# A four-stage fused kernel: attention's weighted sums taken from fp32 probabilities and values, with VectorE's and GpSimd's work re-ordered by key range

## The chip, the cores and the metric

One core of one Trainium2 chip runs the whole program. The metric is the time of one execution in microseconds of device time; the figure compared is the median over runs. Engines are named as in the profile: PE (TensorE's matmuls), PEld (its weight loads), DVE (VectorE), ACT (ScalarE), POOL (GpSimd), SP (SyncE, which issues DMAs here).

## The reference

Four layers one after the other, each followed by a layer norm, on x of shape [8, 512, 128] in fp32: banded attention, a routed feed-forward with 16 experts (4 per token), a linear attention with decay, and a routed feed-forward with 8 experts (2 per token). The change touches the first layer alone:

```python
qkv = jnp.einsum('bld,ed->ble', xn, w_qkv).reshape(B, L, 3, H, HD)      # H = 16 heads of HD = 8
scores = jnp.einsum('bhqd,bhkd->bhqk', q, k) / jnp.sqrt(jnp.float32(HD))
band = jnp.abs(idx[:, None] - idx[None, :]) <= WINDOW // 2              # 16 keys to either side
scores = jnp.where(band[None, None], scores, -jnp.inf)
attn = jax.nn.softmax(scores, axis=-1)
out = jnp.einsum('bhqk,bhkd->bhqd', attn, v)
return residual + jnp.einsum('bld,ed->ble', out, w_out)
```

## The kernel before, in words

The engines' programs are written by hand, one block per engine, and they meet only at semaphores, so the order of the code is the order on each engine. Attention runs over 8 batches; `over_attention` writes batches 0 and 1 out, loops over batches 2 to 5, and writes 6 and 7 out. The argument `prev` of `body` is 0 for batch 0, 1 for batch 1, and 2 from batch 2 on, when the routing of batch b - 2 runs beside attention of batch b. `nxt` says that there is a batch b + 1 to prepare.

A batch has five key ranges ("range" below, `w` in the code): 128 keys each (`WIN`) and 112, 96, 96, 96 and 112 queries (`NQ`), 512 in all. The 16 heads stand in 4 groups `g` of 4 heads `t`. For each range:

- PE makes transposed scores in `t_bank` for groups 0 and 1, later 2 and 3 (`scores_t`: products of `kst` and `qst`, then the mask and the row maximum from `lay` and `mov`). A second form of the scores (`scores`, in `s_bank`) serves only for the maxima: DVE reduces them (`max_of`, L798) and splits them (`split_max`), PE turns them (`turn_max`) and ACT lays them out (`lay_max`, L1224).
- ACT takes the exponential twice, into fp32 (`prob`, L1229) and into bf16 (`prob_hi`, L1230). The low part `prob_lo`, the difference, is formed by DVE for groups 0 and 2 (`prob_low`, L804) and by POOL for groups 1 and 3 (`low_of`, L595).
- PE forms weighted sums and denominators (`weighted`, L1527): for each group five rounds of four products, one round per operand pair: high probabilities with high and with low values, low probabilities with high values, and both parts with a block of ones. The four products of a round are the four heads; each has 128 rows and 32 columns of the array, at column position 32 t. All add up in the bank `avbank`.
- DVE divides (`divide`: reciprocal L824, product L825) and counts `ao_ready`, for which the next range's first `weighted` waits.

The order on PE in a range is: `scores_t` of groups 0 and 1, `scores` (ranges 0, 1 and 4), `weighted` of the range before for groups 2 and 3, other work, `scores_t` of groups 2 and 3, other work, `weighted` of this range for groups 0 and 1, `turn_max`, other work. The other work is the next batch's projections in fp32 (`stacks`, L1448, eight per batch of 512 columns, each followed by an ACT cast L1210 and a DVE merge L780), its values, the output projection of the batch before (L1538), and the transposes and logits of its routing (L1616, L1622). DVE also normalises (L987), ranks (`weigh`, `place`), and POOL issues 16 indirect DMAs per batch that scatter the rows of batch b - 2 into the experts' regions (`scatter`, L634), and makes the low parts of the experts' weights (L621).

The values are kept in bf16, high and low, in `v2`; DVE makes the low part from PSUM (`value_low`, L790, five instructions per batch).

After the last batch SP fills the experts' regions' tails (L474) and waits for the scatters; then the first expert stage begins.

## Time and profile before

| | us |
|---|---|
| median of 3 runs | 1188.61 (1185.93 to 1189.94) |
| the profiled execution | 1178.28 |
| its span, first to last instruction | 1176.3 |
| attention's stretch, first weighted sum to last | 49.0 to 416.1 |

The span is what the engines' rows add up in; the profiled execution's own time has 2.0 us around it. The profile cuts the span into rows by engine, line and tile; "idle before" is time in which the engine had nothing running before an instruction of that group, with what ended it. A PE instruction's end is modelled, so the start-to-start distance of PE rows says more than their durations.

### The profile page before, as it was taken

The page shows a single profiled execution, that of the slowest core. Times are in us where ns is not written, and L with a number is a line of the kernel's source. Part 1 is how long each engine was busy: PE and PEld are TensorE (multiplying, and loading weights), DVE is VectorE, ACT ScalarE, POOL GpSimd, SP SyncE. Part 2 cuts the span into 40 slices and gives each one's busy share as a digit, 9 for nine tenths or more (in the row PEclk, how much of TensorE's full clock was granted, in tenths as well). Part 3 has the DMA queues.
Part 4 walks back from the last instruction along what each step waited for, and adds up shares of the span by engine and source line. Part 5 has one row for each costly group of instructions (what it writes and reads, how often), then busy time and mean ns, then how long its engine had stood idle before and what let it go on. Part 6 is the DMA issues. An engine that isn't in the chain of part 4 may idle for free.

```text
span 1176.3 us, 36298 instructions
## 1 busy us (share of the span) xinstructions
PE 816.6 (69%) x12246; PEld 626.6 (53%) x12247; DVE 746.2 (63%) x2119; ACT 548.4 (47%) x1350; POOL 639.9 (54%) x645
## 2 busy tenths in 40 slices
PE   3889787687887620888888788825756618999920
PEld 1456454455545520766767676614544517988820
DVE  4677878587776750556555666547887635666656
ACT  2577656555565610544444445502323215666623
POOL 1145477585856875355545555524767662555533
PEclk9898868778787655899899999967676758999975
DMA  6011111111111213322223332232342222222233
GB/s 187 12 30 38 33 45 48 30 54 38 56 36 43 61 56 102 69 60 60 62 61 65 67 68 64 54 108 75 99 137 93 75 79 61 64 59 52 54 122 111
DMA packets 135796, 79.02 MB, mean 67 GB/s; under 512 B 104338, under 2 KB 116793, under 8 KB 135696
## 3 DMA queue, kind: packets, MB, share of 16 engines
q1 hardware_dynamic: 121808, 50.97, 17.6%
q0 software_dynamic: 13312, 25.31, 6.8%
q8 instruction: 71, 1.16, 0.4%
q10 hardware_dynamic: 576, 1.34, 0.3%
q14 instruction: 29, 0.24, 0.1%
HBM read 32.34 MB, written 32.63 MB: 55 GB/s over the span
## 4 chain that ended last, share of the span: by engine, by line
PE 46%; issue 15%; DVE 14%; ACT 7%; POOL 6%; another core or an unknown queue 5%; SPq 3%; DMA 2%; ACTq 1%; DVEq 0%; POOLq 0%
PE avbank L1679 5%; PE proj L1679 5%; POOL xs L634 4%; PE proj L1448 3%; PE t L1660 3%; PE s L1658 2%; PE t L1659 2%; PE t L1658 2%; ACT act_out L1334 2%; PE t L1513 2%; PE s L1659 2%; PE t L1724 2%; PE s L1660 2%; PE avbank L1527 2%
## 5 line engine op out<-in xcount | busy, mean ns | idle before, releaser
L700 POOL DMA_INDIRECT yt<-ysb,to_now x224 | 235.2, 1050 | 240.8 <-ACT ysb L1321 181.2
L634 POOL DMA_INDIRECT xs<-x1p,sidx x192 | 194.3, 1012 | 55.0 <-issue 47.2
L944 DVE CAST h_hi<-act_out 128x512 bf16<-128x512 f32 x152 | 72.5, 477 | 146.2 <-ACT act_out L1334 123.6
L595 POOL TENSOR_TENSOR prob_lo<-prob,prob_hi 128x384 bf16<-128x384 f32 (+1 forms) x80 | 78.7, 984 | 91.8 <-ACT prob_hi L1230 90.6
L1658 PE MATMUL s<-xt,w_hi 128*128 128x256 bf16 x296 | 82.8, 280 | 54.3 <-DMA xt<-xs 45.6
L945 DVE TENSOR_TENSOR h_lo<-act_out,h_hi 128x512 bf16<-128x512 f32 x152 | 107.8, 709 | 5.2
L1229 ACT ACTIVATE prob<-t 128x384 f32<-128x384 f32 (+1 forms) x160 | 82.0, 513 | 36.1 <-PE t L1513 34.7
L1334 ACT ACTIVATE act_out<-t,b_sb 128x256 f32<-128x256 f32 x152 | 62.0, 480 | 60.0 <-remote 51.2
L1679 PE MATMUL avbank<-w_hi,h_hi 128*128 x448 | 84.8, 222 | 4.9 <-issue 3.6
L1659 PE MATMUL s<-xt,w_hi 128*128 128x256 bf16 x296 | 82.8, 280 | 6.5 <-issue 6.5
L1660 PE MATMUL s<-xt,w_lo 128*128 128x256 bf16 x296 | 82.9, 280 | 5.5 <-issue 5.5
L1679 PE MATMUL proj<-w_hi,h_hi 128*128 x448 | 82.8, 221 | 5.1 <-DVE h_lo L945 2.5
L1679 PE MATMUL avbank<-w_lo,h_hi 128*128 x448 | 82.1, 220 | 2.8 <-issue 2.8
L1659 PE MATMUL t<-xt,w_hi 128*128 128x256 bf16 x296 | 81.8, 277 | 1.6 <-issue 1.6
L1679 PE MATMUL avbank<-w_hi,h_lo 128*128 x448 | 82.5, 220 | 0.6 <-issue 0.6
L1658 PE MATMUL t<-xt,w_hi 128*128 128x256 bf16 x296 | 81.8, 277 | 1.3 <-issue 1.2
L1660 PE MATMUL t<-xt,w_lo 128*128 128x256 bf16 x296 | 81.8, 276 | 0.9 <-issue 0.8
L1230 ACT ACTIVATE prob_hi<-t 128x384 bf16<-128x384 f32 (+1 forms) x160 | 82.3, 514 | 0.0
L1679 PE MATMUL proj<-w_lo,h_hi 128*128 x448 | 81.1, 220 | 1.6 <-issue 1.6
L1679 PE MATMUL proj<-w_hi,h_lo 128*128 x448 | 81.0, 220 | 0.5 <-issue 0.5
L804 DVE TENSOR_TENSOR prob_lo<-prob,prob_hi 128x384 bf16<-128x384 f32 (+1 forms) x80 | 71.4, 892 | 15.1 <-ACT prob_hi L1230 12.5
L798 DVE TENSOR_REDUCE nm<-s 128x8 f32<-128x512 f32 x64 | 41.2, 685 | 49.6 <-PE s L1476 49.4
(230 smaller groups left out, 2396.5 us busy)
## 6 DMA issues: line engine op xcount, KB each, us to landing
w_raw<-w_all SPq DMA_DIRECT2D x56, 256.0 KB
gat<-yt SPq DMA_DIRECT2D x8, 1024.0 KB
gat<-yt SPq DMA_DIRECT2D x8, 512.0 KB, 4.5
yt<-ysb,to_now POOLq DMA_INDIRECT x224
xs<-tail_rows SPq DMA_DIRECT2D x24, 129.0 KB
xs<-x1p,sidx POOLq DMA_INDIRECT x192
out<-ow SPq DMA_DIRECT2D x8, 256.0 KB, 2.4
xt<-xs SPq DMA_TRANSPOSE x112, 2.9
```

The source lines that it names most:

```text
L595: pool.tensor_tensor(prob_lo[:, g, 0:width], prob[:, g, 0:width], prob_hi[:, g, 0:width], ALU.subtract).then_inc(low_odd, 1)
L634: pool.indirect_dma_start(out=xs[n][:, :], out_offset=bass.IndirectOffsetOnAxis(sidx[:, par, at:at + 1], 0), in_=x1p[:, par, t, k, :], in_ ...
L700: pool.indirect_dma_start(out=yt[n][:, :], out_offset=bass.IndirectOffsetOnAxis(to_now[:, u, s:s + 1], 0), in_=ysb[:, u, s, :], in_offset= ...
L944: ch.link(dve.tensor_copy(h_hi[:, par, c, :], act_out[:, par, c, :]))
L945: dve.tensor_tensor(h_lo[:, par, c, :], act_out[:, par, c, :], h_hi[:, par, c, :], ALU.subtract).then_inc(split_done[n], 1)
L1229: nc.scalar.activation(prob[:, g, 0:width], t_bank[g % 2][:, 0:width], ACT.Exp, scale=SCALE)
L1230: nc.scalar.activation(prob_hi[:, g, 0:width], t_bank[g % 2][:, 0:width], ACT.Exp, scale=SCALE).then_inc(exp_done, 1)
L1334: ins = nc.scalar.activation(act_out[:, par, c, :], h_bank[2 * par + c // 2][:, (c % 2) * TILE:(c % 2 + 1) * TILE], ACT.Gelu, bias=b1_sb[: ...
L1658: pe.matmul(dst, w_h, xt[:, u, 0, :], start=True, stop=False)
L1659: pe.matmul(dst, w_h, xt[:, u, 1, :], start=False, stop=False)
L1660: return pe.matmul(dst, w_l, xt[:, u, 0, :], start=False, stop=True)
L1679: ins = pe.matmul(dst, x[:, par, c, rows], w, start=(n == 1 and c == 0 and m == 0 and k == 0), stop=True, skip_group_check=True)
```

## The change

The probabilities are kept only as `prob` in fp32, the values only as `vf` in fp32, and the ones too. ACT takes one exponential per group instead of two; `prob_low` on DVE, `low_of` on POOL and `value_low` on DVE are gone; `weighted` issues two rounds of four products with fp32 operands instead of five with bf16 ones. `exp_done` takes the place of the semaphores of the low parts. DVE's list is written in another order: `divide` comes first in each range, the maxima and the other work behind it, and `weigh` and `place` go from range 0 to the end of range 1's list. POOL's scatters go from ranges 1 to 4 (one row block each) to ranges 2, 3 and 4 (one, one and two row blocks); `rstd_of_y` and `rstd_of` come ahead of them.

```diff
@@ tiles
-        v2 = sb("v2", [P, 2, NW, 4, VT], BF16)
-        one_of = sb("one_of", [P, G * 5 * HD], BF16)
+        vf = sb("vf", [P, 2, NW, 4, G * VG])
+        one_of = sb("one_of", [P, G * 5 * HD])
-        prob_hi = sb("prob_hi", [P, G, 4 * P], BF16)
-        prob_lo = sb("prob_lo", [P, G, 4 * P], BF16)
@@ gpsimd
-            def low_of(win, w, g):
-                pool.wait_ge(exp_done, G * win + g + 1)
-                width = 4 * NQ[w]
-                pool.tensor_tensor(prob_lo[:, g, 0:width], prob[:, g, 0:width], prob_hi[:, g, 0:width],
-                                   ALU.subtract).then_inc(low_odd, 1)
...
                 for w in range(NW):
-                    low_of(b * NW + w, w, 1)
-                    if prev == 2 and w > 0:
-                        if w == 1:
+                    if w == 1 and prev:
+                        rstd_of_y(b)
+                    if w == 2 and nxt2:
+                        rstd_of(b + 2)
+                    if prev == 2 and w > 1:
+                        if w == 2:
                             pool.wait_ge(slots_ready[0], b - 1)
                             pool.wait_ge(x1_spread, b - 1)
                             apart(pool)
-                        scatter(0, par, w - 1, range(0, K0 // 2))
-                    low_of(b * NW + w, w, 3)
...
+                        for t in ((0,), (1,), (2, 3))[w - 2]:
+                            scatter(0, par, t, range(K0))
@@ vector
-            def value_low(b, par):
...
-            def prob_low(win, w, g):
...
                 for w in range(NW):
                     win = b * NW + w
-                    if w < 2:
-                        max_of(b, 1, 2 * w)
-                        max_of(b, 1, 2 * w + 1)
-                    if w == 1:
-                        split_max(b, 1)
-                    if w == 4 and nxt:
-                        max_of(b + 1, 0, 0)
-                        max_of(b + 1, 0, 1)
-                    prob_low(win, w, 0)
                     if w > 0 or prev:
                         beside = None
                         if w == 0 and prev == 2:
                             beside = lambda: take_ranks(0, b - 2, rk_ps)
                         divide(win - 1, (w - 1) % NW, par if w > 0 else 1 - par, beside)
...
+                    if w < 2:
+                        max_of(b, 1, 2 * w)
+                        max_of(b, 1, 2 * w + 1)
+                    if w == 0:
+                        stack(0, 1)
+                    if w == 1:
+                        if prev:
+                            residual(b - 1)
+                        split_max(b, 1)
+                        stack(2)
+                        if prev:
+                            residual_stats(b - 1)
+                        stack(3)
+                        if prev == 2:
+                            weigh(0, b - 2)
+                            place(0, b - 2, par)
...
@@ scalar
-                nc.scalar.activation(prob[:, g, 0:width], t_bank[g % 2][:, 0:width], ACT.Exp, scale=SCALE)
-                nc.scalar.activation(prob_hi[:, g, 0:width], t_bank[g % 2][:, 0:width], ACT.Exp,
+                nc.scalar.activation(prob[:, g, 0:width], t_bank[g % 2][:, 0:width], ACT.Exp,
                                      scale=SCALE).then_inc(exp_done, 1)
@@ tensor
-                pe.wait_ge((low_even, low_odd)[g % 2], 2 * win + g // 2 + 1)
+                pe.wait_ge(exp_done, G * win + g + 1)
                 nq = NQ[w]
                 ones = one_of[:, 4 * HD * g:4 * HD * g + 4 * HD]
-                for dst, part, x in ((num_ps, 0, prob_hi), (num_ps, 4 * HD, prob_hi), (num_ps, 0, prob_lo),
-                                     (den_ps, None, prob_hi), (den_ps, None, prob_lo)):
+                for dst in (num_ps, den_ps):
                     for t in range(4):
                         ins = pe.matmul(dst[32 * t:32 * t + 32, 0:nq],
-                                        ones if part is None else value_block(par, w, t, g, part),
-                                        x[:, g, t * nq:(t + 1) * nq],
-                                        start=g == 0 and x is prob_hi and part == 0, stop=True,
+                                        value_block(par, w, t, g) if dst is num_ps else ones,
+                                        prob[:, g, t * nq:(t + 1) * nq],
+                                        start=g == 0 and dst is num_ps, stop=True,
                                         skip_group_check=True, tile_position=(0, 32 * t))
```

On DVE this is what stands at ranges 0 and 1 of batch 6 (`qst<-hi,cf,proj` is a stack's merge, `nm<-s` the maxima, `rden` and `ao_t` the division, `msum` to `sidx` are `weigh` and `place`). Before, range 0:

```order
L798 TENSOR_REDUCE nm<-s 128x2x4 x2
L804 TENSOR_TENSOR prob_lo<-prob,prob_hi 128x448
L863 TENSOR_TENSOR r<-avbank,cf 128x64
L824 RECIPROCAL rden<-avbank 128x112
L97 ISA
L825 TENSOR_TENSOR ao_t<-avbank,rden 128x112
L804 TENSOR_TENSOR prob_lo<-prob,prob_hi 128x448
L780 SCALAR_TENSOR_TENSOR qst<-hi,cf,proj 128x512 x2
L870 TENSOR_REDUCE msum<-mask 128x16
```

And in the changed kernel, ranges 0 and 1 of the same batch:

```order
L831 TENSOR_TENSOR r<-avbank,cf 128x64
L792 RECIPROCAL rden<-avbank 128x112
L97 ISA
L793 TENSOR_TENSOR ao_t<-avbank,rden 128x112
L772 TENSOR_REDUCE nm<-s 128x2x4 x2
L765 SCALAR_TENSOR_TENSOR qst<-hi,cf,proj 128x512 x2
L792 RECIPROCAL rden<-avbank 128x112
```

The division has moved ahead of the maxima, and `weigh` no longer follows range 0's merges; it stands behind range 1's last merge, ahead of range 2's division.

On PE this is range 1 of batch 6 from the scores for the maxima (`s`) to the output projection (`wo`) and the next scores (`t`); between them stand range 0's groups 2 and 3. Before:

```order
L1476 MATMUL s<-kst,qst 32x64 x64
L1527 MATMUL avbank<-prob_hi,v 32x112 x8
L1527 MATMUL avbank<-prob_lo,v 32x112 x4
L1527 MATMUL avbank<-prob_hi,one_of 32x112 x4
L1527 MATMUL avbank<-prob_lo,one_of 32x112 x4
L1527 MATMUL avbank<-prob_hi,v 32x112 x8
L1527 MATMUL avbank<-prob_lo,v 32x112 x4
L1527 MATMUL avbank<-prob_hi,one_of 32x112 x4
L1527 MATMUL avbank<-prob_lo,one_of 32x112 x4
L1538 MATMUL proj<-wo,ao_t 128x128 x4
L1506 MATMUL t<-qst,kst 128x96 x8
```

And the same place in the changed kernel:

```order
L1439 MATMUL s<-kst,qst 32x64 x64
L1489 MATMUL avbank<-prob,vf 32x112 x4
L1489 MATMUL avbank<-prob,one_of 32x112 x4
L1489 MATMUL avbank<-prob,vf 32x112 x4
L1489 MATMUL avbank<-prob,one_of 32x112 x4
L1500 MATMUL proj<-wo,ao_t 128x128 x4
L1469 MATMUL t<-qst,kst 128x96 x8
```

Twenty bf16 products per group have become eight fp32 products; their place among PE's other work is the same.

On POOL, ranges 1 to 4 of batch 6 in the changed kernel (each `xs` is an indirect DMA of `scatter`, `w_lo` and `x1p` are low parts, `rstd` a power):

```order
L613 TENSOR_TENSOR rstd<-ve,cf 128x4
L608 TENSOR_TENSOR w_lo<-w_raw,w_hi 128x512
L619 DMA xs<-x1p,sidx 69632x258 x4
L608 TENSOR_TENSOR w_lo<-w_raw,w_hi 128x512
L619 DMA xs<-x1p,sidx 69632x258 x4
L626 TENSOR_TENSOR x1p<-x1f,x1p 128x4x128
L608 TENSOR_TENSOR w_lo<-w_raw,w_hi 128x512
L619 DMA xs<-x1p,sidx 69632x258 x8
```

Before, the same 16 stood in ranges 1 to 4, one or two between two `prob_lo` instructions; now eight stand in one run in range 4.

## Rows read from the trace of the kernel before

**Rows 1.** The page: busy time by engine, and PE's granted clock in 40 slices.

```profile
PE 816.6 (69%) x12246; PEld 626.6 (53%) x12247; DVE 746.2 (63%) x2119; ACT 548.4 (47%) x1350; POOL 639.9 (54%) x645
...
PEclk9898868778787655899899999967676758999975
```

**Rows 2.** Windows, one per batch: length, busy time by engine, clock, DMA share, GB/s.

```profile
44.00:83.00 39.00, 33.04 (x945) 20.58 (x946) 28.27 (x59) 27.61 (x68) 16.55 (x16) 0.91 0.11 30
83.00:124.30 41.30, 36.06 (x895) 23.39 (x891) 31.86 (x92) 27.12 (x65) 18.21 (x17) 0.86 0.10 29
124.30:174.00 49.70, 39.58 (x904) 26.28 (x903) 38.74 (x101) 29.68 (x72) 34.54 (x33) 0.81 0.15 45
174.00:227.40 53.40, 39.70 (x891) 24.82 (x887) 38.09 (x102) 29.22 (x71) 34.73 (x33) 0.79 0.14 42
227.40:278.20 50.80, 41.95 (x896) 27.40 (x895) 38.68 (x101) 29.43 (x71) 34.50 (x33) 0.74 0.15 44
278.20:327.50 49.30, 39.56 (x906) 26.00 (x904) 38.08 (x101) 29.86 (x72) 34.73 (x33) 0.81 0.15 45
327.50:377.00 49.50, 38.76 (x895) 24.88 (x894) 32.00 (x88) 29.08 (x71) 33.27 (x32) 0.81 0.15 45
377.00:417.90 40.90, 27.52 (x641) 20.60 (x640) 30.34 (x75) 24.04 (x58) 32.36 (x31) 0.58 0.17 52
```

**Rows 3.** Groups by form, batches 2 to 6 (124.3 to 377).

```profile
L1527 PE MATMUL avbank<-prob_hi,v 128*32 128x96 bf16 x480 | 17.4, 233 | 14.9 <-DVE ao_t L825 13.9 <-POOL prob_lo L595 0.8
...
L824 DVE RECIPROCAL rden<-avbank 128x112 f32<-128x112 f32 x10 | 8.5, 848 | 0.0
...
L825 DVE TENSOR_TENSOR ao_t<-avbank,rden 128x112 f32<-128x112 f32 x10 | 2.7, 274 | 0.3
```

**Rows 4.** Timeline of PE at full clock: start us, us, instructions merged.

```profile
285.84 0.22 PE L1527 MATMUL avbank<-prob_lo,v 128*32 128x112 bf16 x4
285.89 0.22 PE L1527 MATMUL avbank<-prob_hi,one_of 128*32 128x112 bf16 x4
285.94 0.22 PE L1527 MATMUL avbank<-prob_lo,one_of 128*32 128x112 bf16 x4
...
286.34 1.16 PE L1538 MATMUL proj<-wo,ao_t 128*128 128x128 f32 x8
```

**Rows 5.** Timeline of PE at half clock.

```profile
307.81 1.73 PE L1622 MATMUL proj<-g_route,y 128*128 128x16 f32 x8
...
309.61 0.29 PE L1527 MATMUL avbank<-prob_lo,v 128*32 128x96 bf16 x4
309.69 0.29 PE L1527 MATMUL avbank<-prob_hi,one_of 128*32 128x96 bf16 x4
```

**Rows 6.** The page's costliest groups: the instructions that the change removes.

```profile
L595 POOL TENSOR_TENSOR prob_lo<-prob,prob_hi 128x384 bf16<-128x384 f32 (+1 forms) x80 | 78.7, 984 | 91.8 <-ACT prob_hi L1230 90.6
...
L1230 ACT ACTIVATE prob_hi<-t 128x384 bf16<-128x384 f32 (+1 forms) x160 | 82.3, 514 | 0.0
...
L804 DVE TENSOR_TENSOR prob_lo<-prob,prob_hi 128x384 bf16<-128x384 f32 (+1 forms) x80 | 71.4, 892 | 15.1 <-ACT prob_hi L1230 12.5
```

**Rows 7.** Groups by form, whole span: the values' low part.

```profile
L790 DVE TENSOR_TENSOR v<-proj,v 128x128 bf16<-128x128 f32 x40 | 8.6, 279 | 0.0
```

**Rows 8.** Timeline of DVE: the same four instructions, beside POOL's work and alone.

```profile
300.12 2.38 DVE L987 TENSOR_SCALAR x1f<-y,mv,rstd 128x128 f32<-128x128 f32 x4
...
424.71 1.28 DVE L987 TENSOR_SCALAR x1f<-y,mv,rstd 128x128 f32<-128x128 f32 x4 [1.07 <-POOL rstd L628]
```

**Rows 9.** Window on DVE that holds `weigh` and `place` of one batch.

```profile
285.59:288.13 2.54, 2.22 (x10) 1.00 0.10 19
```

**Rows 10.** Timeline of POOL, the last two scatters of the stage.

```profile
460.60 0.95 POOL L634 DMA_INDIRECT xs<-x1p,sidx  x1 [0.30 <-issue]
461.85 0.96 POOL L634 DMA_INDIRECT xs<-x1p,sidx  x1 [0.30 <-issue]
```

**Rows 11.** The chain that ended last, at the end of the stage.

```profile
466.55 2.05 DMA xs<-tail_rows
```

More of the change, by code:

```diff
@@ L34 @@
 NQ = [QLO[w + 1] - QLO[w] for w in range(NW)]
-VG, VT = 9 * HD, 4 * 9 * HD
+VG = 4 * HD
 EPS = 1e-5
@@ L359, in program, with value_at, value_block @@
         x_tiles = x_in.rearrange("b (t p) d -> p (b t) d", p=P)
-        def value_at(par, w, part):
-            return v2[:, par, w, :, :].rearrange("p t (g x) -> p t g x", g=G)[:, :, :, part:part + HD]
-        def value_block(par, w, t, g, part):
-            return v2[:, par, w, t, 8 * HD * g + part:8 * HD * g + part + 4 * HD]
+        def value_at(par, w):
+            return vf[:, par, w, :, :].rearrange("p t (g x) -> p t g x", g=G)[:, :, :, 0:HD]
+        def value_block(par, w, t, g):
+            return vf[:, par, w, t, 3 * HD * g:3 * HD * g + 4 * HD]
         def more_groups(eng, n):
@@ L622, in body @@
                                            w0_hi[:, bass.ds(at, CH)], ALU.subtract).then_inc(lo_done, 1)
-                        if prev == 2 and w > 0:
-                            scatter(0, par, w - 1, (3,))
             def rstd_of_y(count):
@@ L782, in prep_stack @@
                                          op1=ALU.add).then_inc(stack_ready, 1)
-            def value_low(b, par):
-                for part, (bank, ws) in enumerate(((proj[1], range(0, 4)), (proj[0], range(4, 5)))):
-                    dve.wait_ge(v_high, 2 * b + part + 1)
-                    for w in ws:
-                        at = (w % 4) * P
-                        ins = dve.tensor_tensor(value_at(par, w, 4 * HD),
-                                                bank[:, at:at + P].rearrange("p (t g d) -> p t g d", t=4, g=G),
-                                                value_at(par, w, 0), ALU.subtract)
-                    ins.then_inc(v_copied, 1)
             def max_of(b, phase, g):
@@ L1106, in body @@
                             prep_stats(b + 2)
-                    if w == 3 and nxt2:
-                        prep_xhat(b + 2)
-                    if w == 4 and nxt:
-                        max_of(b + 1, 0, 2)
-                        max_of(b + 1, 0, 3)
-                        split_max(b + 1, 0)
-                    prob_low(win, w, 2)
-                    if w == 0:
-                        stack(0, 1)
-                    if w == 0 and prev == 2:
-                        weigh(0, b - 2)
-                        place(0, b - 2, par)
-                    if w == 1:
-                        stack(2, 3)
-                    if w == 2 and prev:
-                        normalise(b - 1, i - 1 + par, 1 - par, prev == 2)
-                    if w == 2:
-                        stack(5, 6)
+                        stack(5)
+                        if prev:
+                            normalise(b - 1, i - 1 + par, 1 - par, prev == 2)
+                        stack(6)
                     if w == 3:
                         stack(7)
-                    if w == 3 and prev:
-                        take_logits(0, b - 1)
-                    if w == 4 and nxt:
-                        value_low(b + 1, 1 - par)
-                    if prev and w == (4 if nxt else 3):
-                        choose(0)
-                        mark(0)
+                        if nxt2:
+                            prep_xhat(b + 2)
+                        if prev:
+                            take_logits(0, b - 1)
+                        if not nxt:
+                            choose(0)
+                            mark(0)
+                    if w == 4 and nxt:
+                        for g in range(G):
+                            max_of(b + 1, 0, g)
+                        split_max(b + 1, 0)
+                        if prev:
+                            choose(0)
+                            mark(0)
                     if w == 4 and not nxt:
@@ L1149, in _ @@
             max_of(0, 0, 1)
-            value_low(0, 0)
             max_of(0, 0, 2)
```

29 lines of the change are left out of this document (7 added, 22 removed).

## The prediction

> **What bounds the kernel now.** I read the page first. PE is the busiest engine, but at 69% of the span, and its granted clock moves between the levels [rows 1]. The change lives in attention, so I cut the trace by batch, each window beginning at the division that opens it [rows 2]. Batches 0 and 1, without routing beside them, take 39.0 and 41.3 us; batches 2 to 6 take 49.7, 53.4, 50.8, 49.3 and 49.5 us, 252.7 together; batch 7, which prepares nothing, takes 40.9. In batches 2 to 6 PE is busy for 39.9 us in the mean and idle for 10.6; DVE is busy for 32 to 39 of some 50 us, POOL for 34.4, ACT for 29.5. No engine is full. What ends each wait is a chain that goes round: PE, ACT's exponentials, the low parts on DVE and POOL, PE's sums, DVE's division. Of PE's waits ahead of the sums in those batches, 13.9 of 14.9 us end at the quotient [rows 3]. The granted clock there is 0.74 to 0.81, that is, some four tenths of the time are at 1.2 GHz and the rest at 2.4; in batches 0 and 1, where PE is idle for only 6.0 and 5.2 us, it is 0.91 and 0.86, and in batch 7, with 13.4 idle, 0.58.
>
> So PE's work in a batch, put at full clock, is 39.9 x 0.79 = 31.6 us for batches 2 to 6; likewise 30.1 for batch 0, 31.0 for batch 1 and 16.0 for batch 7.
>
> **What the sums cost PE.** At full clock the rounds of four 112-query products start 0.05 us apart (285.84, 285.89, 285.94) [rows 4]: 112 columns at 2.4 GHz are 0.047 us, so the four column positions stream together. At half clock a 96-query round takes 0.08 us [rows 5], which is 96 columns at 1.2 GHz. A group's queries over a batch are 512, four groups give 2048 columns: 0.85 us at full clock per round kind. Five kinds are 4.3 us, with some 0.003 us per start (20 groups x 5) 4.6.
>
> No fp32 product with 32 columns is in the trace. The nearest row is the output projection, fp32 on the whole array: its four matmuls are eight records in 1.16 us [rows 4]; take off the last record's tail and eight remain some 0.11 us apart, where 128 columns once are 0.053. So an fp32 matmul is two records, each of which streams its columns twice. The records of one matmul follow each other on the same array columns, so the second waits for the first. Records start in order. Then position 32's first record can run beside position 0's second, but its own second waits again: four matmuls cost four streams of two passes, not one. **I take this value:** a group costs 8 x 2 passes, a batch 16 x 0.85 = 13.7 us, with starts 14.1. Against 4.6 that is **9.5 us more per batch** at full clock, 19 at half. Bounds: if all four positions' records ran together, 8 passes, 6.8 + 0.2 = 7.0 us, 2.4 more. If no two records overlapped, 32 passes, 27.3 + 0.8 = 28.1 us, 23.5 more. Weight loads: the logits' records with 16 columns are 0.21 us apart at half clock (1.73 us for eight) [rows 5], which is their 128-column fp32 weights; 32 columns are a quarter, 0.05 us at half clock, under a stream of 0.16, so hidden.
>
> **What goes from the others.** ACT's second exponential: 160 of 514 ns, 82.3 us, 10.3 per batch. DVE's low parts: 71.4 us, 8.9 per batch. POOL's: 78.7 us, 9.8 per batch [rows 6]. The values' low parts, 40 x 279 ns, 1.1 per batch on DVE [rows 7]. In batches 2 to 6 ACT falls from 29.5 to 19, DVE from 37 to 27, POOL from 34 to 25. Besides, DVE instructions stretch beside POOL's: the same four normalising instructions took 2.38 us between POOL's work and 1.28 alone [rows 8]. None of this is time by itself; it shortens the links between PE's pieces. With the division first in the list, the quotient is ready about 1.3 us after the sums (0.85 + 0.27 and two hand-overs [rows 3]), under PE's next scores and a projection, so the 13.9 us of waiting [rows 3] mostly end.
>
> **What the new order adds.** `weigh` and `place`, 2.5 us from the first of their instructions to the last [rows 9], stand behind range 1's last merge, and range 2's division behind them; behind it wait PE's next sums. By my estimate, range 1's last merge ends 1.6 us into range 2, so the quotient comes at 1.6 + 2.5 + 1.1 = 5.2 us; PE has until then its first scores (0.7), groups 2 and 3 (1.3), two projections (1.1 each) and the second scores (0.7), 4.9 us: 0.3 to 0.6 us of wait, where range 0 loses its own. POOL's eight scatters of range 4 take 8 x 1.25 = 10 us and end up to 3 us later than now. After batch 7 this moves the last scatter, 461.85 us now, 1.25 after the one before it [rows 10], toward the last tail's DMA at 466.55 [rows 11], for which SP waits anyway: 1 us at most is left of it. That work is hidden by the tails' DMAs; without them it would cost 3. The scatters' own number is unchanged.
>
> **The sum.** In batches 2 to 6 PE has 31.6 + 9.5 = 41.1 us at full clock. Links: I go through the five ranges with the removed instructions left out and find waits for the transposed maxima (ranges 0 and 4), for the normalised input's cast (0.35), for the transpose of range 3 (0.85) and for the last maxima (0.6 to 1), 3 to 4 us in all; I take 4, below the 5.2 and 6.0 of batches 0 and 1 now, which have more ACT work. The clock is my choice: 0.91 is the highest that a batch has now, PE waits less in the changed kernel, and I take 0.97. 41.1 / 0.97 + 4 = 46.4 us; five batches are 232, against 252.7: **20.7 less**. Batch 0: (30.1 + 9.5) / 0.97 + 3.5 = 44.3, 5.3 more. Batch 1: 40.5 / 0.97 + 3.5 = 45.3, 4.0 more. Batch 7: (16.0 + 9.5) / 0.77 + 11 = 44.1, 3.2 more; the clock there is my choice between its 0.58 and 0.91. Start and end: 0.5 more. Sum: **7.7 us less**. The profiled execution has 1178.3 us (span 1176.3), so 1170.6; against the median of the runs, 1188.6, it is **1181 us**, 0.65% less. A change within 0.3%, some 3.6 us, can't be told from none here.
>
> **Rivals.**
> 1. *The clock stays where it is* (slower). 0.85 for batches 2 to 6, 0.9 and 0.87 for 0 and 1, 0.62 for 7: 52.4 us each (8.5 more in five), then 8.5, 8.8 and 11 more, with 1 at the ends: 38 us more, 1227. It decides from a clock of 0.884 in batches 2 to 6, where 41.1 / c + 4 is today's 50.5. For it: the clock fell in each of them; against it: it was highest where PE waited least.
> 2. *fp32 products at different columns don't overlap* (slower). 23.5 instead of 9.5 more per batch on an engine that then has no idle time to give: about 14 x 8 = 112 us more than forecast, 1293. Against it: the bf16 rounds [rows 4] overlap, and the eight fp32 records pass without a gap.
> 3. *All four positions run together* (faster). 7.1 us less per batch on PE, but then links bind: some 45 us for each of batches 2 to 6, 41, 42 and 42 for the others, in all 24 less than now: 1164.
> 4. *The order gives it back*: `place` and the unoverlapped scatters make range 2's quotient and the next weights' low part 1 to 2 us late per batch; six batches, 6 to 12 us: 1187 to 1193, no change that can be told.
>
> On rival 3 the Trainium skill has a rule (TensorE: Matmul & The Clock Gate, Measured speedup vs the span model): packed tiles span one matmul and about 4 ns per further tile. The bf16 rounds [rows 4] agree, 0.05 us for four. Taken for fp32 it gives rival 3; I hold that a matmul of two records on one tile breaks it. The same page (The mechanism) says that a weight load overlaps running matmuls only where the row group differs. All four positions share their rows, and yet the loads don't lengthen those rounds. By that rule the sum would be nearer rival 2's.
>
> **Chances.** Forecast 0.50, rival 1 0.20, rival 2 0.10, rival 3 0.08, rival 4 0.12. Faster by over 0.3%: three quarters of the forecast's (its own range is 1163 to 1198) and rival 3's, 0.46. The same: 0.14, from the forecast's edge and half of rival 4. Slower: 0.40. The range of 8 in 10 runs from 1156, below rival 3, to 1228, just over rival 1's clock; rival 2 lies outside.
>
> **What would show it.** In the changed profile: one round of four fp32 products of 96 queries takes about 0.33 us at full clock (0.16 for rival 3, 0.65 for rival 2). Clock of batches 2 to 6 at 0.95 or more (rival 1: 0.85 or less). PE idle 4 us in such a batch. PE's waits ahead of the sums for `ao_t` below 5 us in batches 2 to 6, and the one left in range 2. DVE at about 27 us of busy time per batch. Wrong it would be above all through the price of a round, since each 0.1 us per group is 2 us per batch; then through the clock.

## The result: 1.35% slower, and where the time went

The changed kernel takes **1203.8 us** (median of four runs, 1201.5 to 1204.9), the kernel before beside it 1187.3 (1182.4 to 1189.9): ratio **1.0135, 95% interval 1.0095 to 1.0176**. I had forecast 1181. The time lies in the range, the direction is wrong.

The same windows as [rows 2], each to the division that closes the batch, in the changed kernel (window, length, then busy time of PE, PEld, DVE, ACT and POOL with instructions, PE's granted clock, DMA share, GB/s):

```profile
42.00:79.30 37.30, 34.20 (x867) 21.84 (x866) 18.95 (x41) 21.11 (x47) 5.63 (x5) 0.95 0.12 31
79.30:115.60 36.30, 34.10 (x818) 22.74 (x819) 24.34 (x76) 19.62 (x45) 7.78 (x7) 1.00 0.11 32
115.60:169.40 53.80, 41.31 (x818) 27.32 (x816) 26.93 (x87) 22.48 (x51) 23.37 (x23) 0.84 0.14 42
169.40:229.80 60.40, 42.22 (x815) 27.03 (x814) 26.92 (x86) 21.82 (x51) 23.34 (x23) 0.75 0.13 38
229.80:283.20 53.40, 41.25 (x819) 26.56 (x817) 26.90 (x86) 21.82 (x51) 23.32 (x23) 0.81 0.14 42
283.20:336.80 53.60, 41.22 (x818) 26.03 (x816) 27.07 (x87) 21.82 (x51) 23.35 (x23) 0.81 0.14 42
336.80:389.20 52.40, 40.58 (x821) 25.82 (x819) 24.76 (x73) 22.02 (x51) 22.26 (x22) 0.84 0.14 42
389.20:431.00 41.80, 28.31 (x567) 19.91 (x561) 18.83 (x68) 17.04 (x40) 22.62 (x22) 0.72 0.18 53
```

The changed kernel behaves in two ways. Batches 0 and 1, in which nothing is scattered, end at 115.6 us where they ended at 124.3 [rows 2]: 8.7 us won. Batches 2 to 6 take 273.6 us in place of 252.7: 20.9 lost. Batch 7 takes 0.9 more. Attention ends 13.1 us later (431.0 against 417.9). The profiled executions lie 23 us apart, the medians 16.6: the profiled one of before was 9 us under its own median, and of the 23 us some 10 lie behind the first expert product (at 485.45 us, before at 472.49), in stages that the change doesn't touch.

Batch 4, cut at its divisions (the same columns), shows which range it is:

```profile
237.70:246.70 9.00, 8.83 (x132) 5.03 (x132) 8.41 (x27) 5.20 (x12) 2.61 (x3) 1.00 0.13 33
246.70:253.20 6.50, 4.36 (x98) 2.98 (x98) 5.44 (x20) 2.64 (x6) 2.77 (x3) 1.00 0.17 50
253.20:273.30 20.10, 12.65 (x198) 8.79 (x192) 2.94 (x9) 4.29 (x9) 16.28 (x17) 0.68 0.23 70
273.30:283.20 9.90, 8.04 (x223) 5.27 (x223) 6.22 (x25) 3.13 (x10) 0.96 (x1) 0.61 0.05 17
```

The stretch of 20.1 us holds the starts of 13 of POOL's 16 scatters: it took 11.4 us before in four of the five batches. In the other batches the loss lies in this stretch or in the closing one: 12.8 and 18.2 us in batch 2, 18.7 and 18.7 in batch 3, 18.6 and 11.8 in batch 5, 12.0 and 14.6 in batch 6 (before 9.2 to 11.4 and 10.5 to 13.5). DVE is busy for 2.9 and ACT for 4.3 of its 20 us. Here are their timelines in it, DVE, then ACT, then POOL (start, us, engine, line, operation, tiles, and in brackets the idle time ahead and what is taken to have ended it):

```profile
260.01 0.21 DVE L798 TENSOR_TENSOR lg<-proj,c_route 128x64 f32<-128x64 f32 x1
273.28 0.76 DVE L792 RECIPROCAL rden<-avbank 128x96 f32<-128x96 f32 x1 [13.05 <-remote]
...
263.23 0.98 ACT L1193 ACTIVATE prob<-t 128x448 f32<-128x448 f32 x2 [0.67 <-PE t L1476]
276.18 0.98 ACT L1193 ACTIVATE prob<-t 128x448 f32<-128x448 f32 x2 [11.98 <-remote]
...
264.64 0.98 POOL L619 DMA_INDIRECT xs<-x1p,sidx  x1 [0.17 <-issue]
265.93 0.96 POOL L619 DMA_INDIRECT xs<-x1p,sidx  x1 [0.30 <-issue]
267.20 0.96 POOL L619 DMA_INDIRECT xs<-x1p,sidx  x1 [0.30 <-issue]
...
273.51 0.96 POOL L619 DMA_INDIRECT xs<-x1p,sidx  x1 [0.31 <-issue]
```

The reciprocal divides a bank whose last product ended at 265.99 us; it starts 7.3 us later. The exponentials' scores were complete at 268.0; ACT takes them up at 276.2. "remote" is what the page writes where it finds nobody in the trace that released the engine. This happens while POOL issues eight scatters in a row, their starts 1.26 us apart. The chain that ended last, which the page follows back from the last instruction, has one piece for it:

```profile
260.30 12.95 another core or an unknown queue
```

and from 115 to 420 us, that is over batches 2 to 6 and most of 7, the waits say the same of both engines (engine and instruction, then who released it, us in all, times, longest). Before, the division has one such wait, of 1.0 us, and the exponentials none; ACT's layout of the maxima has six, 14.1 us in all and at most 2.5:

```profile
ACT prob L1193 <- remote: 56.7, 13, 12.0
DVE rden L792 <- remote: 46.3, 8, 13.1
```

The price of the sums, on which I had put most weight, stands in the rounds of one fp32 product kind, 112 queries at full clock, then 96 at half:

```profile
285.60 0.38 PE L1489 MATMUL avbank<-prob,one_of 128*32 128x112 f32 x8
285.79 0.38 PE L1489 MATMUL avbank<-prob,vf 128*32 128x112 f32 x8
285.98 0.38 PE L1489 MATMUL avbank<-prob,one_of 128*32 128x112 f32 x8
...
264.48 0.55 PE L1489 MATMUL avbank<-prob,vf 128*32 128x96 f32 x8
264.81 0.55 PE L1489 MATMUL avbank<-prob,one_of 128*32 128x96 f32 x8
```

A round starts every 0.19 us; 112 columns are 0.047 us at 2.4 GHz [rows 4], so it costs four passes for all four positions together, and 0.33 at half clock, four times [rows 5]'s 0.08. That is rival 3's price, 2.4 us a batch, not my 9.5.

### The profile page after: what moved, and what is told of

Its sections match the earlier page's. It is cut to its first block, busy times and chain, and to the rows that moved or that the text cites. A ratio compares the mean times of both kernels' runs of the same rounds, so it can differ in the third digit from the quotient of the medians.

```text
span 1199.4 us, 34606 instructions
## 1 busy us (share of the span) xinstructions
PE 825.0 (69%) x11606; PEld 630.4 (53%) x11607; DVE 664.4 (55%) x1999; ACT 488.0 (41%) x1190; POOL 553.4 (46%) x565
## 4 chain that ended last, share of the span: by engine, by line
PE 46%; issue 17%; DVE 12%; another core or an unknown queue 8%; ACT 6%; POOL 4%; SPq 3%; DMA 2%; ACTq 1%; DVEq 0%; POOLq 0%
PE avbank L1641 5%; PE proj L1641 4%; PE proj L1411 4%; PE avbank L1489 3%; POOL xs L619 3%; PE t L1622 2%; PE s L1620 2%; PE s L1622 2%; PE t L1620 2%; PE t L1621 2%; PE t L1686 2%; PE s L1621 2%; PE t L1476 2%; ACT act_out L1297 2%
## 5 line engine op out<-in xcount | busy, mean ns | idle before, releaser
L619 POOL DMA_INDIRECT xs<-x1p,sidx x192 | 187.7, 978 | 63.6 <-issue 55.6
L1193 ACT ACTIVATE prob<-t 128x384 f32<-128x384 f32 (+1 forms) x160 | 73.5, 509 | 100.3 <-remote 60.5
L608 POOL TENSOR_TENSOR w_lo<-w_raw,w_hi 128x512 bf16<-128x512 f32 (+1 forms) x32 | 37.1, 1161 | 158.8 <-ACT w_hi L1268 158.3
L1620 PE MATMUL t<-xt,w_hi 128*128 128x256 bf16 x296 | 82.9, 280 | 6.8 <-issue 6.8
L1621 PE MATMUL t<-xt,w_hi 128*128 128x256 bf16 x296 | 83.1, 281 | 3.9 <-issue 3.9
L1489 PE MATMUL avbank<-prob,vf 128*32 128x96 f32 (+1 forms) x1280 | 67.5, 282 | 13.5 <-DVE ao_t L793 9.0
L1297 ACT ACTIVATE act_out<-s,b_sb 128x256 f32<-128x256 f32 x152 | 60.8, 480 | 34.4 <-remote 19.1
L792 DVE RECIPROCAL rden<-avbank 128x96 f32<-128x96 f32 (+1 forms) x40 | 31.8, 795 | 73.8 <-remote 46.3
```

Of the source, the lines that this page charges most:

```text
L619: pool.indirect_dma_start(out=xs[n][:, :], out_offset=bass.IndirectOffsetOnAxis(sidx[:, par, at:at + 1], 0), in_=x1p[:, par, t, k, :], in_ ...
L1193: nc.scalar.activation(prob[:, g, 0:width], t_bank[g % 2][:, 0:width], ACT.Exp, scale=SCALE).then_inc(exp_done, 1)
L1297: ins = nc.scalar.activation(act_out[:, par, c, :], h_bank[2 * par + c // 2][:, (c % 2) * TILE:(c % 2 + 1) * TILE], ACT.Gelu, bias=b1_sb[: ...
L1489: ins = pe.matmul(dst[32 * t:32 * t + 32, 0:nq], value_block(par, w, t, g) if dst is num_ps else ones, prob[:, g, t * nq:(t + 1) * nq], st ...
L1620: pe.matmul(dst, w_h, xt[:, u, 0, :], start=True, stop=False)
L1621: pe.matmul(dst, w_h, xt[:, u, 1, :], start=False, stop=False)
```

## The experiments

Theory A, as I first held it: eight scatters in a row hold DVE and ACT up. B: the later place of weights, row numbers and scatters costs the time by the order itself. C: the fp32 sums or the clock do. All ratios are against the kernel before on the same chip, with 95% intervals. "2 to 6" is the time from the last division of batch 1 to that of batch 6, from the starts of the reciprocals in each trace (before: 252.7; changed: 273.6). The expectations name the versions by these short labels; e8 to e10, each executed once, add scatters or memsets in batches 0 and 1; e11, e12 and e16 to e18 vary what stands between scatters.

| run | ratio | 2 to 6, us |
|---|---|---|
| changed kernel | 1.0135 (1.0095 to 1.0176) | 273.6 |
| e1, paced by the exponentials | 1.0157 (1.0112 to 1.0202) | 273.8 |
| e3, early and paced | 1.0108 (1.0058 to 1.0158) | 271.7 |
| e4, fp32 sums alone | 1.0049 (1.0016 to 1.0082) | 269.7 |
| e6, before, late scatters | 1.0459 (1.0413 to 1.0504) | 309.5 |
| e2, changed, memset between scatters | 0.9807 (0.9770 to 0.9845) | 235.2 |
| e15, fp32 sums alone, memset between | 0.9846 (0.9810 to 0.9882) | 243.5 |
| e13, early and paced, memset between | 0.9915 (0.9883 to 0.9946) | 248.3 |
| e14, before, memset between | 1.0241 (1.0201 to 1.0280) | 271.9 |
| e19, changed, memset in range 4 only | 0.9955 (0.9932 to 0.9978) | 249.1 |
| e5, before, division first | 1.0080 (1.0052 to 1.0107) | 258.4 |

**Pacing the scatters.** In ranges 2 to 4 of the changed kernel:

```diff
-    for t in ((0,), (1,), (2, 3))[w - 2]:
-        scatter(0, par, t, range(K0))
+    for g in range(G):
+        pool.wait_ge(exp_done, G * (b * NW + w) + g + 1)
+        apart(pool)
+        for t in ((0,), (1,), (2, 3))[w - 2]:
+            scatter(0, par, t, (g,))
```

> The changed kernel with its scatters in the same three ranges, but each (in range 4 each pair) behind a wait for the exponentials of one group of heads, so that no eight stand in a row. Theory A (an unbroken run of scatters holds up VectorE and ScalarE): the 12 us waits of ScalarE's exponentials and of VectorE's reciprocal in range 4 go, range 4 takes about 12 us where it took 18 to 20, and 5 batches give back 6 to 8 us each: 1164 to 1176 us. Rival B (the later place in the program of the weights, the row numbers and the scatters costs the time, however they are spaced): within 5 us of 1204. Rival C (the fp32 sums or the clock cost it): within 5 us of 1204 as well, with the waits in range 4 still there.

1.0157: no gain. The longest waits of ACT and DVE with no releaser shrank from 12 and 13 us to 6.2 and 6.5. In batches 2 to 6 there were as many as ever, 26, and their sum fell from 120 to 79 us, yet the batches took as long: these waits are a sign of the loss and not its measure. Of the 80 scatters, 60 still started under 1.5 us after the one ahead: the exponentials themselves were late, and POOL, once it was behind, found its waits fulfilled. Theory A in this form (a long run is what costs) fell, and B and C were open again.

**Weights and row numbers early again, four scatters in each range.** The pacing above with `w - 1` as the tile in ranges 1 to 4, and `weigh` and `place` behind `stack(0, 1)` of range 0.

> The changed kernel with weights and row numbers back in range 0 and four scatters in each of ranges 1 to 4, each behind one group's exponentials. Theory A: no run of scatters anywhere, so 1160 to 1175 us, and no more than 4 us from the version that is only paced. Rival B: the order is undone too, so this one alone is fast, 1165 to 1180, while the version that is only paced stays near 1204. Rival C: near 1204.

1.0108, so B explains at most a part. Here too 54 scatters stood under 1.5 us apart, and the divisions of ranges 2 and 3 came 10 to 13.5 and 12 to 13 us behind the one ahead, where before they came 8 to 9 and 9 to 11.

**The fp32 sums alone.** DVE's and POOL's order of before with the low parts left out, since nothing reads them; in their place on POOL a wait:

```diff
-    low_of(b * NW + w, w, 1)
+    pool.wait_ge(exp_done, G * (b * NW + w) + 2)
+    apart(pool)
```

> The kernel before with the sums from fp32 probabilities and values alone: VectorE's and GpSimd's orders as before without the low parts (GpSimd still waits for the same two groups' exponentials, then issues two, one and one scatters). Theory A with the round price as the trace after shows it (four passes, the four column positions together): 15 to 25 us under before, 1162 to 1172 us. Rival C (the sums themselves cost what the removal brings): 1185 or more. Rival D (VectorE's late division is what the sums wait for, so that the gain needs the new order): 1176 to 1187.

1.0049, on rival C's side of what was expected. But the loss isn't spread evenly. Batch 1 falls from 41.3 to 35.8 us, batches 2 to 6 rise from 50.5 to 53.9 in the mean. In this trace I first saw that PE, too, is held up; the same rhythm stands in the kernel before, at 214.98 to 216.43 us, with two and three products at a time and 0.52 us idle between. This is PE's timeline beside three scatters (starts 261.69, 262.98 and 264.25):

```profile
262.25 0.27 PE L1447 MATMUL s<-kst,qst 32*32 32x64 bf16 x5 [0.23 <-issue]
262.98 0.27 PE L1447 MATMUL s<-kst,qst 32*32 32x64 bf16 x5 [0.46 <-issue]
263.70 0.27 PE L1447 MATMUL s<-kst,qst 32*32 32x64 bf16 x6 [0.45 <-issue]
264.43 0.28 PE L1447 MATMUL s<-kst,qst 32*32 32x64 bf16 x5 [0.46 <-issue]
```

These products wait for no semaphore, yet PE takes five or six of them every 0.73 us and idles for 0.46 between. So what is short there is no data that the program waits for; what it is, is argued at the end. And the low parts on POOL had done a second thing in the kernel before, which I had not seen: they stood between the scatters.

**The kernel before with the late scatters.** Its bf16 sums and low parts kept, `weigh` and `place` moved to range 1, the scatters 4, 4 and 8 in a row ahead of `low_of` in ranges 2 to 4.

> The kernel before, bf16 sums and low parts kept, with weights and row numbers in range 1 and the scatters 4, 4 and 8 in a row at the start of ranges 2, 3 and 4. Theory A: the run of eight stalls VectorE and ScalarE here too, about 6 to 9 us of range 4 in each of 5 batches, and GpSimd's low parts of the odd groups wait 10 us behind it besides: 1225 to 1245 us. Rival C (only the fp32 sums are to blame): within 6 us of 1187. My prediction's own price for the order was 0.3 to 3 us a batch: 1189 to 1202.

1.0459, 4.6%, some 54 us, the largest loss of all, with no fp32 sum in it: rival C is not needed. Its size is no measure of the scatters' effect, though, for the low parts of the odd groups now stand behind the scatters on POOL: in batches 2 to 6 PE waits 38.8 us for them ahead of the sums, where before it waited 0.8. The effect looked for is DVE's wait with no releaser, in batch 4 across POOL's scatters from 284.66 to 294.5:

```profile
296.13 1.29 DVE L793 TENSOR_REDUCE nm<-s 128x8 f32<-128x512 f32 x2 [16.12 <-remote]
```

**A memset between the scatters.** Same ranges, same order, one more instruction on POOL behind each:

```diff
-    scatter(0, par, t, range(K0))
+    for k in range(K0):
+        scatter(0, par, t, (k,))
+        pool.wait_ge(spaced, 16 * (b - 2) + 4 * t + k + 1)
+        apart(pool)
+        pool.memset(spare[:, :], 0.0).then_inc(spaced, 1)
```

`spare` is 128 x 512 fp32 and nothing reads it.

> The changed kernel with a memset of 128 x 512 on GpSimd behind each scatter of the batches' loop, so that no two scatters stand back to back; weights, row numbers and scatters keep their ranges. Theory D (while GpSimd makes the descriptors of one scatter after another, the other engines' queues are hardly served, and they catch up in the gaps between): the stalls of 6 to 8 us on VectorE and ScalarE in range 4 fall to 1 to 3 us, and the time to between 1.000 and 1.010 of the kernel before on the same chip, where the changed kernel stood at 1.0135. Rival E (each scatter costs the others its own microsecond wherever it stands): no change, 1.012 to 1.018. Rival F (more work on GpSimd makes the scatters late for the next batch's rows): over 1.02.

0.9807: better than theory D allowed, and the fastest version of the study (1153.9 us beside 1175.1). POOL in range 4:

```profile
255.06 0.96 POOL L625 DMA_INDIRECT xs<-x1p,sidx  x1 [0.16 <-POOL spare L608]
256.02 0.54 POOL L608 MEMSET spare<- 128x512 f32 x1
256.72 0.97 POOL L625 DMA_INDIRECT xs<-x1p,sidx  x1 [0.17 <-POOL spare L608]
257.69 0.54 POOL L608 MEMSET spare<- 128x512 f32 x1
```

The scatters still take 0.96 us, but start 1.67 us apart, so that POOL is busy longer (27.5 us of batch 4, not 23.3), and DVE and ACT stand no more: in batches 2 to 6 none of their waits is without a releaser. PE's gaps are fewer but not gone. Of its gaps of 0.2 us or more that the timeline puts to "issue", batches 2 to 6 have some 26 here (17 us), 43 in the changed kernel (29 us) and 20 in the kernel before (12 us). Batches 2, 4 and 6:

```profile
116.60:162.00 45.40, 38.00 (x828) 24.75 (x826) 29.44 (x86) 22.11 (x52) 26.17 (x31) 0.93 0.14 42
...
214.50:261.80 47.30, 39.75 (x820) 26.48 (x819) 29.03 (x87) 21.96 (x51) 27.45 (x34) 0.90 0.14 43
...
309.00:351.80 42.80, 36.83 (x828) 23.85 (x827) 25.18 (x74) 21.89 (x52) 30.81 (x38) 0.98 0.17 51
```

The clock came back with it, 0.86 to 0.98 where the changed kernel had 0.75 to 0.84: the low clock followed PE's standing and is not needed as a cause of its own.

**Scatters and plain work where there were none.** 16 scatters of constant rows to a scratch table in each of batches 0 and 1, 4, 4 and 8 in a row; as the control 16 memsets at the same places; and the scatters in the kernel before:

```diff
+    if prev != 2 and w > 1:
+        extra("scatter", (4, 4, 8)[w - 2])      # control: "work"
```

> The changed kernel with 16 scatters of constant rows to a scratch table of their own added in each of batches 0 and 1, which have none, at the places where batches 2 to 6 have theirs (4, 4 and 8 in a row in ranges 2 to 4). Batches 0 and 1 took 37.3 and 36.3 us without them. If scatters hold the other engines up (theories D and E), each of the two takes 8 to 17 us more. If the 53 us of batches 2 to 6 come from what else these do (ranks, weights, row numbers, the residual's rows), no more than 2 us more.

> The control: the changed kernel with 16 memsets of 128 x 512 on GpSimd in each of batches 0 and 1, at the same places. If it is the descriptors and not a busy GpSimd that holds the others up, batches 0 and 1 stay within 1.5 us of 37.3 and 36.3. If a busy GpSimd is enough (its later sums and low parts are what is waited for, or a port shared with VectorE), they grow by as much as with the scatters.

> The kernel before with the same 16 added scatters in batches 0 and 1 (41.0 and 41.3 us without them), 4, 4 and 8 in a row at the start of ranges 2 to 4. Theories D and E: 12 to 20 us more in each, since GpSimd's low parts of the odd groups wait behind them too. If only the fp32 sums suffer from scatters: no more than 3 us more.

Batches 0 and 1 with the scatters:

```profile
42.00:97.10 55.10, 44.40 (x875) 27.29 (x874) 18.05 (x41) 21.53 (x47) 21.42 (x21) 0.75 0.13 40
97.10:152.90 55.80, 43.35 (x818) 27.91 (x819) 24.44 (x76) 19.69 (x45) 23.52 (x23) 0.78 0.13 40
```

and with the memsets:

```profile
42.00:80.80 38.80, 36.40 (x873) 23.20 (x872) 19.39 (x41) 21.41 (x47) 13.83 (x21) 0.89 0.11 30
80.80:117.40 36.60, 34.24 (x818) 22.82 (x819) 26.59 (x77) 19.60 (x45) 15.94 (x23) 1.00 0.11 32
```

Busy times of DVE and ACT differ by 2.2 us at most; the batches with scatters are 16.3 and 19.2 us longer than those with memsets. PE has 27 gaps of the kind above (17 us) in the two batches with scatters, and none in the two with memsets. Whole executions took 1224.7 us with the scatters and 1195.7 with the memsets, one each, beside a median of 1175.1 for the kernel before. The memsets themselves add 0.3 us to batch 1; batch 0, whose window opens at a fixed 42.0 us, has 38.8 here and 37.3 to 39.4 in the versions that add nothing there. 16 scatters at 1.26 us are 20.2 us: unspaced, each costs the batch about what it takes. A busy POOL as such costs next to nothing, with one limit of this control: eight memsets in a row take 4.6 us, eight scatters 9.8. The clock fell to 0.75 and 0.78 here as well. In the kernel before the same scatters bring batches 0 and 1 from 41 to 63.5 and 55.5 us (1206.0 us in all, one execution). Of these 37 us, 14 are PE's plain waits for POOL's low parts, which stand behind the scatters there; but DVE also stands once for 16.5 us with no releaser, so the effect isn't bound to the fp32 sums.

The Trainium skill (SBUF — State Buffer, SBUF: two separate sides) has DVE and GpSimd exclude each other on a shared port pair and says that PE and ACT "never wait on anyone". The trace doesn't agree if one reads the stalls as that lock: ACT waits up to 12 us and PE idles 0.46 us at a time beside the same scatters, and the memsets, POOL operations too, lengthen DVE's own busy time in batch 1 from 24.3 to 26.6 us, but hardly the batch.

**What in the memset frees the others.** It was cut to 128 x 1, and replaced by eight empty instructions.

> The changed kernel with the spacer cut to a memset of 128 x 1 behind each scatter (the 128 x 512 one took 0.54 us and gave 0.981 of the kernel before). Theory D1 (what frees the other engines is that GpSimd does any operation of another kind between two scatters, however short): near 0.981, 0.975 to 0.988. Theory D2 (what frees them is the time of the gap, in which the queues catch up): the gap is some 0.1 us in place of 0.54, so little is won: 1.000 to 1.015.

> The changed kernel with eight empty instructions behind each scatter and no other work. D1: empty instructions are no operation of the engine, so 1.005 to 1.016, with the stalls of 6 to 8 us in range 4 still there. D2: if the scatters' starts move apart to 1.6 us or more, as with the memsets, near 0.981; if they don't move, it tells nothing of D2.

1.0163 (1.0128 to 1.0198) and 1.0169 (1.0132 to 1.0205). D1 fell: POOL did another operation between any two scatters, and nothing was won. In both traces the scatters start 1.26 us apart as ever; the small memset fits into the gap of 0.3 us that was there:

```profile
266.93 0.96 POOL L628 DMA_INDIRECT xs<-x1p,sidx  x1 [0.19 <-issue]
267.89 0.12 POOL L597 MEMSET spare<- 128x1 f32 x1
268.19 0.96 POOL L628 DMA_INDIRECT xs<-x1p,sidx  x1 [0.19 <-issue]
```

The empty instructions didn't move the starts, so that run says nothing of D2; the small memset speaks for it.

**How wide the gap must be.** The memset at 128 x 224, 128 x 384 and 128 x 1024:

> The changed kernel with a memset of 128 x 224 behind each scatter, 0.25 to 0.3 us, so that the starts of two scatters come to stand about 1.35 to 1.45 us apart, between the 1.26 of the changed kernel and the 1.67 of the one at 0.981. If the other engines' gain grows with the gap, 0.990 to 1.008; if there is a step below 1.4 us, near 0.981; above it, near 1.015.

> The changed kernel with a memset of 128 x 384 behind each scatter, about 0.42 us, so that two scatters start some 1.55 us apart. 1.43 us gave 1.020 of the kernel before, 1.67 us 0.981. If there is a step between, this one lies near one of the two, 0.978 to 0.990 or 1.012 to 1.022; if the gain grows with the gap, 0.995 to 1.005.

> The changed kernel with a memset of 128 x 1024 behind each scatter, about 1.1 us, so that the starts stand some 2.2 us apart. If the gain goes on with the gap: 0.970 to 0.980. If 1.67 us is enough and more only makes GpSimd late (16 x 2.2 = 35 us, and four sums of 1.2 us with four low parts, of a batch of 45): 0.980 to 0.995.

| starts apart (median), us | memset, us | ratio | 2 to 6, us |
|---|---|---|---|
| 1.26 | none | 1.0135 (1.0095 to 1.0176) | 273.6 |
| 1.43 | 0.30 | 1.0198 (1.0145 to 1.0252) | 281.6 |
| 1.56 | 0.43 | 1.0052 (1.0020 to 1.0085) | 263.8 |
| 1.67 | 0.54 | 0.9807 (0.9770 to 0.9845) | 235.2 |
| 2.10 | 0.96 | 0.9966 (0.9938 to 0.9995) | 241.8 |

Neither a clean step nor a slope from the origin: 1.43 us is no better than no spacer: the scatters' run grows longer and frees nobody; between 1.43 and 1.67 some 46 us of the five batches are won; beyond that nothing more is won, and POOL gets late. With 2.1 us the last scatter ahead of the experts starts at 455.4 us, with 1.67 at 440.2, in the changed kernel at 475.9.

**Only range 4, or all?** The memset behind the eight scatters of range 4 alone.

> The changed kernel with the 128 x 512 memset behind the eight scatters of range 4 alone; the four and four of ranges 2 and 3 stay 1.26 us apart. If the run of eight is what costs: at least three quarters of the 3.3% between 1.0135 and 0.981 come back, 0.981 to 0.989. If every scatter at 1.26 us costs alike, half: 0.992 to 1.002.

0.9955. Of the 3.3% between the changed kernel and the spaced one, 1.8% come back, by half of the scatters; of the 38.4 us between their traces in batches 2 to 6, 24.5. The time fits scatters that all cost alike, the trace rather a run of eight that costs somewhat more; it is not three quarters of the loss by either.

**The parts of the change, once the gaps are there.** The fp32 sums alone with the memset; the kernel before with it; the early place with it; and the division first by itself in the kernel before.

> The fp32 sums alone (VectorE's and GpSimd's order of the kernel before; 1.005 of it without the spacers) with the memset behind each scatter. Theory D: the loss of that version was the scatters standing together once the low parts between them are gone; it falls to 0.975 to 0.985. Rival (it was the late division or the sums' own price): stays at 1.000 or above.

> The kernel before with a 128 x 512 memset behind each of its 16 scatters a batch. There two, one and one stand between the low parts, and the trace shows only 2 us waits of ScalarE at the pairs. Theory D: a small gain, 0 to 10 us, 0.992 to 1.000. Rival (the memsets take GpSimd's time, on which the sums of the odd groups wait there): up to 10 us slower, 1.000 to 1.010.

> The version with weights and row numbers in range 0 and four scatters in each of ranges 1 to 4 (1.011 of the kernel before), with the 128 x 512 memset behind each scatter. If the gaps are all that counts, as e2 (0.981) and e15 (0.985) say, the scatters' ranges matter little: 0.975 to 0.988. If the later place in the changed kernel is worth something once the gaps are there, this one stands above 0.984; if it costs something, under 0.977.

> The kernel before with VectorE's division of the last range ahead of the maxima and of the low part in every range, and nothing else. My prediction counted 0.3 to 0.6 us of cost in range 2 and 3 us of gain at the first divisions for the new order. If the order is worth nothing by itself: 0.997 to 1.003. If the early release of the sums' bank is what the fast batches 0 and 1 come from: 0.985 to 0.995. If putting the maxima and low parts later costs: over 1.003.

With the gaps there the sums alone are worth 1.5%: from 1.0049 without the spacer to 0.9846 with it, the same instructions otherwise. All parts together are 0.9807, so the new order adds 0.4%, within what the two intervals leave. The early and paced place gave 0.9915 against 0.9807 for the late one, which is against theory B. It doesn't show that scatters are better late: this version also waits for exponentials ahead of every scatter, and e15, whose scatters are early too with two such waits in a range, has 0.9846. In the kernel before the division ahead of the maxima and the low part lost 0.8%, where I had counted a gain; with it the low parts come later, and which of the two costs was not separated.

The kernel before with the memset was a miss: 1.0241, where I expected 0.992 to 1.010. POOL is busy for 43.8 of the 60.2 us from 227.5 to 287.7, and the sums' weight loads now wait for its low parts (us in all, times, longest; batches 2 to 6, where before it was 1.3 us):

```profile
PEld avbank L1537 <- POOL prob_lo L597: 23.2, 16, 3.5
```

The spacer pays only where POOL has time for it, which the fp32 sums gave.

## Why the prediction was wrong, by its own steps

- **The step that failed** is in "What the new order adds": POOL's scatters were costed by their own 10 us, called hidden behind the tails, and at 0 for everybody else. Shown: 16 close scatters make a batch that had none 16 to 19 us longer than 16 memsets do, and 0.41 us more between the starts of two turns 1.0135 into 0.9807. That is 38 us in batches 2 to 6, more than the whole error of 22.8.
- **"What goes from the others"** came true in busy time: DVE 26.9 us in most batches where I said 27, POOL 23.3 (25), ACT 21.8 (19). But the low parts on POOL were counted as load alone, and they were also the space between scatters. With the sums alone changed (e4) and POOL's 80 gone, batches 2 to 6 lost 17.0 us and batches 0 and 1 won 9.1; with the memsets between the scatters (e15) 2 to 6 won 9.2. The four instructions that I read as running alone in [rows 8], 1.28 us at 424.71, in fact have a scatter of POOL beside them (424.88, 1.09 us), so one scatter beside them doesn't lengthen those four instructions.
- **The price of a round** was mis-sized: 9.5 us a batch taken, 2.4 measured, my lower bound. The second record of a matmul doesn't hold up the other positions. PE's work at full clock, busy time by clock, is 34.1 us in batch 1 (31.0 before) and 33.5 in the mean of 2 to 6 (31.6), 3.1 and 1.9 more. That the time still fell into my range is luck: 7.1 us a batch too much for the rounds stood against scatters that I had put at nothing. The Trainium skill's rule on packed tiles (TensorE: Matmul & The Clock Gate, Measured speedup vs the span model), weighed in the prediction, agrees with these fp32 rounds; I had taken it to break there.
- **Idle time and clock.** I took 4 us of idle and 0.97; batches 2 to 6 had 12 to 18 us idle and 0.75 to 0.84. Batch 1, without scatters, had 2.2 us idle and 1.00, so the reading "the clock is high where PE waits little" holds. Rival 1's sign, a clock of 0.85 or less, came true, but not its time, 1227, nor its reason: with the scatters apart the clock rose to 0.86 to 0.98.
- **The quotient.** PE's waits for it fell from 13.9 to 6.3 us (I said below 5; the row is below), the first division of a batch comes 7.5 us after the last instead of 12. But in the kernel before the early division cost 0.8%. The groups by form of 115.6 to 389.2, the row that answers [rows 3]:

```profile
L1489 PE MATMUL avbank<-prob,vf 128*32 128x96 f32 x480 | 23.8, 272 | 7.2 <-DVE ao_t L793 6.3 <-issue 0.9
```

- **Rival 3** was what the change would have brought with the scatters apart: 1164 us against 1188.6 is 0.979, the spaced version has 0.981. The sum fits in part by luck: it took 45 us for each of batches 2 to 6, where 47.0 were measured, and 42 each for batches 1 and 7, where it was 36.3 and 34.7. **Rival 4** named the scatters, at 1 to 2 us a batch and as lateness of the next weights; the size and the way were both wrong. **Rival 2** is excluded by the rounds.

Left open: by what the other engines are held. PE's rhythm of five products in 0.73 us without a semaphore, and DVE and ACT standing with their inputs ready, point to the supply of instructions or the sequencers; that is argued, not shown. A plain transfer issued by POOL in place of the indirect one wasn't tried, so the issuing of the scatters and their transfers are not told apart either. Batch 3 is 2 to 7 us longer than its neighbours in nearly every version, before included [rows 2]. It closes the first pass of the loop over batches 2 to 5, and PE's first products behind the jump back, the scores of batch 4, wait with no releaser: 3.6 us before, 3.7 and 2.5 in the changed kernel, 4.4 and 2.8 in the spaced one. No version without the loop was run.

## What to carry to other kernels

An instruction that is taken away may have been spacing others: before costing a removal, look at what stands back to back on that engine afterwards, and above all at indirect DMAs of GpSimd. Look in the trace of before at batches that have such DMAs and batches that don't; here batches 2 to 6 were 8 to 12 us longer than batch 1, which was reason enough to test. How much of it was the scatters no run shows; in the spaced version batches 2 to 6 are still 10.7 us longer than batch 1. When an engine's wait has no releaser in the trace and its input is ready, ask what another engine is issuing in those microseconds, and test it by adding that thing where there is none, with plain work as the control.

## What the runs showed of the hardware that I had not expected

- Indirect scatters of 128 rows issued 1.26 us apart hold up DVE, ACT and PE at once: beside a run of eight, DVE and ACT stood up to 13 us, in batch 4 7.3 and 8.2 of them with their inputs ready; at 1.67 us apart they have no such wait, and PE still has gaps, 17 us in place of 29. 1.43 us is no better than 1.26.
- Eight empty instructions or a memset of 0.12 us fit into the 0.3 us between two scatters and don't move their starts.
- Four fp32 products at four column positions cost four passes together: 0.19 us a round of 112 columns at full clock, 0.33 of 96 at half.
